# A two-layer graph network on one core: both ends of the kernel are reordered

## What is computed

```
h  = relu(layernorm(x))                                  # x: (128, 128, 64)
hj = relu(h @ W1a [j]  +  (h[j] - h[k]) @ W1b + b1)      # for each edge j-k, 192 wide
x  = x + (sum over k of mask[j,k] * hj) @ W2 + deg[j] * b2
h  = relu(layernorm(x))
x  = x + (adj @ h) @ W^T
```

## Time and profile before

| | |
|---|---|
| median of 3 runs | 842.91 us (841.57 to 843.62) |
| the profiled execution, its own time | 845.98 us |
| its span, first to last instruction | 844.1 us |
| busy share of the span: PE, PEld, DVE, ACT, POOL | 96%, 85%, 96%, 94%, 72% |
| mean granted TensorE clock | 0.98 of full |
| codes | 0 to 46.3 us |
| tables, until `tables_ready` | 46.3 to 52.1 us |
| loop over graphs, first sum to last gather | 56.9 to 827.3 us |
| tail: last steps and the last store | 827.3 to 844.1 us |

### The profile page before, as it was taken

How to read it: one execution, slowest core, us unless ns; L and a number is a source line. 1 busy time by engine, 2 the same in 40 slices (tenths; PEclk the granted TensorE clock), 3 DMA queues, 4 the chain that set the end, 5 groups by cost and what they waited for, 6 DMA issues and landing times.

```text
span 844.1 us, 26648 instructions
## 1 busy us (share of the span) xinstructions
PE 810.6 (96%) x8242; PEld 715.0 (85%) x8243; DVE 809.9 (96%) x2894; ACT 794.9 (94%) x2246; POOL 611.5 (72%) x1174
## 2 busy tenths in 40 slices
PE   4879999999999999999999999999999999999996
PEld 2447888898889888988998899888988898889884
DVE  6969999999999999999999999999999999999993
ACT  4969999999999999999999999999999999999992
POOL 1966777777777777777777777777777777777762
PEclk8979999999999999999999999999999999999996
DMA  9800000000000000000000000000000000000000
GB/s 337 327 1 2 7 9 21 21 21 15 21 20 21 9 21 21 20 15 21 21 21 9 20 21 21 15 21 20 21 9 21 21 20 14 21 21 21 15 3 21
DMA packets 26705, 27.55 MB, mean 33 GB/s; under 512 B 3520, under 2 KB 24512, under 8 KB 25536
## 3 DMA queue, kind: packets, MB, share of 16 engines
q1 hardware_dynamic: 25488, 25.37, 8.9%
q10 hardware_dynamic: 1072, 0.43, 0.2%
HBM read 21.59 MB, written 4.19 MB: 31 GB/s over the span
## 4 chain that ended last, share of the span: by engine, by line
PE 90%; DVE 4%; issue 2%; ACT 2%; DMA 1%; SPq 0%; ACTq 0%; DVEq 0%
PE ring L414 48%; PE ring L442 8%; PE prep L471 5%; PE post L514 4%; PE post L501 3%; PE post L508 3%; PE post L502 3%; PE prep L479 3%; PE prep L482 2%; PE prep L477 2%; DVE acc L826 2%; PE post L506 2%; DMA x_all<-x_nbf_dram 1%; PE prep L473 1%; DVE onehot_space L812 1%
## 5 line engine op out<-in xcount | busy, mean ns | idle before, releaser
L826 DVE SCALAR_TENSOR_TENSOR acc<-ring,acc 128x384 f32<-128x384 f32 x896 | 488.6, 545 | 0.6
L572 ACT COPY ring<-P 128x384 f32<-128x384 f32 x1024 | 466.6, 509 | 19.3 <-DVE acc L826 11.4
L414 PE MATMUL ring<-PQ,onehot_space 128*128 128x192 f16 x4096 | 417.0, 247 | 4.5 <-ACT ring L572 2.2
L414 PEld LDWEIGHTS ring<-PQ,onehot_space 128*128 128x128 f16 x4096 | 328.0, 99 | 39.4 <-issue 13.5
L922 POOL TENSOR_SCALAR start<-P,spare 128x192 f32<-128x192 f32 x128 | 128.4, 1003 | 134.8 <-ACT P L622 133.8
L946 POOL TENSOR_TENSOR row_space<-row_space 128x192 f32<-128x192 f32 x256 | 153.4, 599 | 25.3 <-ACT row_space L610 8.2
L812 DVE TENSOR_SCALAR onehot_space<-mask_all 128x512 f16<-128x512 f16 x512 | 158.1, 311 | 0.0
L442 PE MATMUL ring<-PQ,owner 128*128 128x384 f16 (+1 forms) x512 | 93.9, 306 | 0.0
L414 PE MATMUL ring<-PQ,onehot_row 128*128 128x192 f16 x768 | 84.3, 246 | 0.5 <-DVE onehot_row L874 0.3
L610 ACT ACTIVATE row_space<-ring 128x576 f32<-128x576 f32 x128 | 83.3, 651 | 0.7 <-PE ring L414 0.7
L826 DVE SCALAR_TENSOR_TENSOR acc<-ring,start 128x384 f32<-128x384 f32 x128 | 71.1, 556 | 5.3 <-PE ring L414 1.3
(11 more groups left out here) (138 smaller groups left out, 1431.9 us busy)
## 6 DMA issues: line engine op xcount, KB each, us to landing
onehot_space<-adj_kbj_dram SPq DMA_DIRECT2D x8, 1024.0 KB, 17.3
adj_again<-adj_kbj_dram SPq DMA_DIRECT2D x128, 64.0 KB, 2.0
x_all<-x_nbf_dram SPq DMA_DIRECT2D x8, 512.0 KB, 19.0
out_dram<-x_all SPq DMA_DIRECT2D x32, 128.0 KB, 1.9
consts<-consts_dram SPq DMA_DIRECT2D x1, 192.0 KB, 2.4
scratch<-w1a_dram ACTq DMA_DIRECT2D x2, 48.0 KB, 4.2
scratch<-w1b_dram ACTq DMA_DIRECT2D x2, 48.0 KB, 6.7
scratch<-b_dram ACTq DMA_DIRECT2D x1, 96.0 KB, 10.1
```

What stands on the lines that cost most here:

```text
L414: last = nc.tensor.matmul(to, hot(s), parts[:, part, H:2 * H], start=False, stop=(part == 1), skip_group_check=True)
L572: return nc.scalar.copy(slots[to][:, bank_], src.unsqueeze(1).broadcast_to([N, PER_BANK, H]))
L826: return nc.vector.scalar_tensor_tensor(sums, slots[to][:, bank_], 0.0, start[:, :, :] if first else sums, ALU.max, ALU.subtract if first ...
```

## The change

At the front: TensorE's products for the scale search come later, behind part 2 and part 3 of the codes, and VectorE's and ScalarE's share of the search moves back with them; mask 2 comes ahead of the first maximum. Four ring writes come ahead of the first pair of table products. The first four one-hots are made before VectorE waits for the last codes, and two small operations trade places with waits. ScalarE runs parts 1 to 3 in a loop of the device and does its first two norms ahead of the scaled weights.

In every step: TensorE's wait for `hm_row_ready` stands between the transposes and the product that needs it.

At the tail: in step 128 VectorE, not GpSimd, adds the three slots of the last graph's owned rows. ScalarE makes the two `h2` of the last two pairs together, in the odd step. The last store is split in two.

```diff
-            sp.wait_ge(y_ready, B // 2)
-            sp.dma_start(out[:, B - STORE:B, :], x_all[:, B - STORE:B, :]).then_inc(stored, 16)
-            sp.wait_ge(stored, 16 * B // STORE)
+            for done in range(B - STORE + 2, B + 1, 2):
+                sp.wait_ge(y_ready, done // 2)
+                sp.dma_start(out[:, done - 2:done, :], x_all[:, done - 2:done, :]).then_inc(stored, 16)
+            sp.wait_ge(stored, 16 * (B // STORE - 1 + STORE // 2))
...
             codes(0)
-            codes(1, range(QUADS // 2))
+            codes(1)
+            codes(2)
 
             pe.wait_ge(largest_ready, 1)
             nc.tensor.matmul(post[0:1, 0:N], to_scale[:, 0:1], ident, start=True,
                              stop=True).then_inc(largest_seen, 1)
-            codes(1, range(QUADS // 2, QUADS))
+            codes(3)
             pe.wait_ge(largest_ready, 2)
             nc.tensor.matmul(post[:, N:N + 1], ones_row[:, :], to_scale[0:1, 1:2], start=True, stop=True).then_inc(largest_seen, 1)
-            with pe.Fori(2, LATE) as g:
+            with pe.Fori(EARLY, LATE) as g:
                 codes(g)
...
                             pe.wait_ge(summed, b * REGULAR)
-                            pe.wait_ge(hm_row_ready, b)
                             if not main:
                                 pe.wait_ge(even_T_ready, pairs(b, u, t, -2))
                             for s in range(PER_BANK):
                                 nc.tensor.matmul(head_ps, acc_space[:, (u - 1) // 2 % 2, s, heads[(u - 1) % 2]], ident, start=(s == 0), stop=False, is_transpose=True)
+                            pe.wait_ge(hm_row_ready, b)
                             last = nc.tensor.matmul(head_ps, row_heads[(u - 1) % 2], ownerT[:, (u - 1) % QUAD, :], start=False, stop=True)
...
-            pe.wait_ge(rows_counted, 1)
-            nc.tensor.matmul(tables[:, 0, :], ones[:, :], rows, start=True, stop=True)
-            nc.tensor.matmul(tables[:, 1, :], rows, ones[:, :], start=True, stop=True).then_inc(rows_summed, 1)
...
             pe.wait_ge(code_kj_ready, B // QUAD)
-            pe.wait_ge(code_jk_ready, B // QUAD)
             write_ring(range(QUADS))
+
+            pe.wait_ge(rows_counted, 1)
+            nc.tensor.matmul(tables[:, 0, :], ones[:, :], rows, start=True, stop=True)
+            nc.tensor.matmul(tables[:, 1, :], rows, ones[:, :], start=True, stop=True).then_inc(rows_summed, 1)
...
-                    if i == 4 and exists(b - 5):
+                    if i == 4 and exists(b - 5) and (u % 2 or exists(b - 1)):
...
-                        k, g = (u - 5) // 2 % 2, (u - 5) % 2
-                        nc.scalar.activation(h2[:, k, 2 * g, :], x_all[:, b - 5, :], ACT.Relu, bias=shift2[:, k, g:g + 1],
-                                             scale=rstd2[:, k, g:g + 1]).then_inc(h2_ready, 1)
+                        k = (u - 5) // 2 % 2
+                        for g in range(2) if not exists(b - 1) else ((u - 5) % 2,):
+                            of = b - 5 - (u - 5) % 2 + g
+                            nc.scalar.activation(h2[:, k, 2 * g, :], x_all[:, of, :], ACT.Relu, bias=shift2[:, k, g:g + 1],
+                                                 scale=rstd2[:, k, g:g + 1]).then_inc(h2_ready, 1)
...
             codes(0)
-            codes(1)
-            codes(2)
+            with nc.scalar.Fori(1, EARLY) as g:
+                codes(g)
+            act.wait_ge(norm1_ready, 1)
+            lead(step, hi=-1)
             act.wait_ge(scale_ready, 1)
             nc.scalar.activation(w_parts[:, 0, :, 0:H], w_pq[:, :].rearrange("p (k h) -> p k h", k=3), ACT.Copy,
                                  scale=to_scale[:, 2:3]).then_inc(first_parts_ready, 1)
-            codes(3)
-            act.wait_ge(norm1_ready, 1)
-            lead(step, hi=-1)
...
             norm1_stats(1)
+            mask(2)
             largest()
-            mask(2)
-            largest_of_rows()
             moments(0)
             norm1_stats(2)
-            scale()
             mask(3)
+            largest_of_rows()
             norm1_stats(3)
             moments(1)
             mask(4)
-            second_parts()
+            scale()
             mask(5)
             norm1_stats(4)
+            second_parts()
             mask(6)
...
             moments(3)
+            dve.wait_ge(code_kj_ready, 1)
+            first_hot()
...
-            dve.wait_ge(p_ready, 1)
-            second_part(0, 0)
-
             dve.wait_ge(rows_summed, 1)
...
+            nc.vector.tensor_copy(row_count[:, :], owned)
+            dve.wait_ge(p_ready, 1)
+            second_part(0, 0)
             dve.wait_ge(owned_sums, 1)
             nc.vector.tensor_scalar(loops[0:1, 0, :], tables[0:1, 3, :], float(LOOPED), None, ALU.mult)
-            nc.vector.tensor_copy(row_count[:, :], owned)
...
+                if not main and b == B:
+
+                    dve.wait_ge(relu_row_ready, B)
+                    sums = relu_rows[(u - 1) % 2][:, 0, :]
+                    nc.vector.tensor_tensor(sums, sums, relu_rows[(u - 1) % 2][:, 1, :], ALU.add).then_inc(half_row_ready, 1)
+                    dve.wait_ge(half_row_ready, B)
+                    nc.vector.tensor_tensor(sums, sums, relu_rows[(u - 1) % 2][:, 2, :], ALU.add).then_inc(hm_row_ready, 1)
...
-            for s in range(SLOTS):
-                last = hot(0, 0, 0, s)
-            last.then_inc(onehot_ready, 1)
             lead(step)
...
-                if exists(b - 1):
+                if exists(b - 1) and exists(b):
 
                     pool.wait_ge(relu_row_ready, b)
```

More of the change, by code:

```diff
@@ L371, in _, with codes @@
                     adj(b + BODY + 1)
-            sp.wait_ge(y_ready, B // 2)
-            sp.dma_start(out[:, B - STORE:B, :], x_all[:, B - STORE:B, :]).then_inc(stored, 16)
-            sp.wait_ge(stored, 16 * B // STORE)
+            for done in range(B - STORE + 2, B + 1, 2):
+                sp.wait_ge(y_ready, done // 2)
+                sp.dma_start(out[:, done - 2:done, :], x_all[:, done - 2:done, :]).then_inc(stored, 16)
+            sp.wait_ge(stored, 16 * (B // STORE - 1 + STORE // 2))
         @block.tensor
         def _(pe):
-            def codes(g, quads=range(QUADS)):
+            def codes(g):
                 pe.wait_ge(mask_ready, g + 1)
-                for q in quads:
+                for q in range(QUADS):
                     quad = g * QUADS + q
@@ L753, in moments, with hot, first_hot @@
                 nc.vector.tensor_tensor(mom[:, 3, b], mom[:, 3, b], mom[:, 2, b], ALU.add).then_inc(moments_ready, 1)
+            def hot(b, u, i, s):
+                return nc.vector.tensor_scalar(onehot[:, hot_of(u), i, s, :, :], code_kj[:, bass.ds(b, QUAD), :],
+                                               2.0 * (SLOTS * i + s) + 1.0, None, ALU.is_equal)
+            def first_hot():
+                for s in range(SLOTS):
+                    last = hot(0, 0, 0, s)
+                last.then_inc(onehot_ready, 1)
             mask(0)
@@ L808, in _ @@
             dve.wait_ge(tables_ready, 1)
-            def hot(b, u, i, s):
-                return nc.vector.tensor_scalar(onehot[:, hot_of(u), i, s, :, :], code_kj[:, bass.ds(b, QUAD), :],
-                                               2.0 * (SLOTS * i + s) + 1.0, None, ALU.is_equal)
             def prepare(b, u, s):
```

## The result

The changed kernel takes 846.83 us (median of 8 runs, 845.11 to 849.21) beside 842.77 (8 runs, 841.57 to 844.04) for the kernel before: 1.0038 times as long, 95% interval 1.0024 to 1.0052. I forecast 841.9 with a range to 843.5, so it went the other way: 4.1 us slower where I had 1.05 faster and gave "slower" a chance of 0.06.

What follows compares the result with a forecast made beforehand. TensorE, VectorE and ScalarE, each 94 to 96% busy, were taken as one full pipeline in the middle, with serial ends. Front 0, middle 0 and tail 1.05 gave 842.91 - 1.05 = 841.86, say 841.9 us; range 839.9 to 843.5.

Steps and rivals of the forecast that it cites:

- The middle: Loop over graphs: a full pipeline whose streamed work the change doesn't alter, moved TensorE wait included; gain 0.
- Rival (d): Every step: TensorE's moved wait between transposes and product opens a gap; at 30 ns a step 845.7; chance 0.05.
- Codes: Front: ScalarE's code copies end 1.25 us earlier, group 4 starting at 28.4 instead of 29.56; bounds 0.3 and 2.0.
- T0: Front: the end of ScalarE's last code copy out of PSUM, 46.31 before, forecast 45.05.
- The 2.76 of idle time: Front: ScalarE's standstill until 18.18, while TensorE waits for the largest weight between two halves of code group 1.
- Ring writes ahead of the tables: Front: four TensorE writes take 1.71 us at clock 0.50, making `owned` 1.71 later against T0, `tables_ready` 0.7 later.
- rival (b): Front: ring writes at full clock take 0.86, `start` comes 0.85 earlier; sum about 1.6, 841.3; chance 0.12.
- GpSimd's `start`: Front, graph 1: done at 62.72 instead of 62.26, so VectorE waits and the 1.65 us won are spent.
- The front: Everything ahead of graph 1: gain 0 in sum, bounds -1.0 and 1.65.
- The tail: From step 128: result copy 0.8 us earlier through VectorE's sums, plus 0.25 from the store; 1.05, bounds 0.5 and 1.8.
- pair norms: Tail: ScalarE's paired norms end near 831.9 and 835.4, before the line 599 copies (near 832.9 and 835.8); counted nothing.
- The halved last store: Tail end: last store, 2.6 us from issue to landing, with half the bytes gains 0.25; skill's estimate 0.15.

Runs made afterwards that it cites:

- e1_wait_only: Kernel before with one edit: TensorE's wait for hm_row_ready stands behind the two transposes; 842.86 us, ratio 0.9996 to the kernel before.
- e5_after_one_more: Changed kernel with one VectorE instruction more (first memset written as two halves); 844.11 us, ratio 0.9997 to the kernel before.
- e7_after_two_more: Changed kernel with two VectorE instructions more (first memset in three pieces); 844.32 us, ratio 1.0000 to the kernel before.
- e10_norm_early_singles: Changed kernel, first memset in halves, GpSimd's last first-layer norm group moved earlier, last second-layer norms one by one; 842.71 us, ratio 0.9984 to the kernel before.
- e12_part_later: Kernel before with VectorE's wait for p_ready and the subtraction behind it moved six instructions later; 847.91 us, ratio 1.0049 to the kernel before.
- e8: Changed kernel with three VectorE instructions more (first memset in four pieces); 844.10 us, ratio 0.9992 to the kernel before.
- e3_front_only: Kernel before with all edits of the front and no other; 847.41 us, ratio 1.0042 to the kernel before.
- e4_all_but_wait: Changed kernel with TensorE's wait for hm_row_ready put back ahead of the transposes; 847.36 us, ratio 1.0046 to the kernel before.

## Why the prediction was wrong, step by step

**The middle** was the step that failed: "the change doesn't alter what any engine streams there", so 0. The products and sums are the same, but their places in VectorE's instruction stream are not. The moved wait was rightly 0. The place of the code cost 3.5 us (0.9997 against 1.0038 with one split memset, with an uncertainty of about 1.4), of which the traces show 2.65 in the middle, 762.07 against 759.42; where the rest lies I can't show, and it may be noise. None of my rivals had this mechanism, so the range left it out. Rival (d) named 845.7, near what was measured, but by a gap at TensorE's wait that `e1_wait_only` doesn't show (0.9996); that nearness is chance. The trace of before could not have shown it: there number 63 falls on the wait in front of these sums, and the sums behind it start on time.

**Codes.** I said T0 would come 1.25 earlier, at 45.05. It came at 45.78, 0.53 earlier:

```profile
19.20 0.59 ACT L568 CAST mask_all<-ring 128x512 f32 x1 [2.00 <-PE ring L392]
...
23.60 0.59 ACT L568 CAST mask_all<-ring 128x512 f32 x1 [0.38 <-PE ring L392]
...
28.76 0.64 ACT L568 CAST mask_all<-ring 128x512 f32 x1
...
33.41 0.59 ACT L568 CAST mask_all<-ring 128x512 f32 x1 [0.34 <-PE ring L392]
...
45.09 0.69 ACT L569 CAST code_jk<-ring 128x512 f32 x1
```

The 2.76 of idle time didn't go; 2.00 of it moved behind group 1, to the wait for mask 2's data, as I had said it would. Group 3 began at 23.60, where I had 23.25, and group 4 at 28.76, where I had 28.4: mask 3 was late by 0.22 and TensorE by the rest. I had then taken 0.15 of the later stalls back; instead one grew, to 0.34 at 33.41, and 0.27 of the 0.80 won by group 4 was lost by 45. The mechanism was right and the size 2.4 times too large, inside my bounds. Over all traces the last copy ends at 46.3 to 46.7 with the old front and at 45.8 to 47.1 with the new one (middle values 46.6 and 46.1), so 0.5 is the typical gain, and two single executions need not show it.

**Ring writes ahead of the tables.** I had 1.71 for them at a granted clock of 0.50. From the last code copy to `owned` the kernel before takes 3.13 (46.31 to 49.44), `e5_after_one_more`, where the clock was at half for the whole stretch, 4.79 (46.68 to 51.47), that is 1.66 more: right for that clock. Five others lie between, at 4.12 to 4.65. But the profiled execution of the changed kernel took 3.09, with its writes at the full clock:

```profile
46.48 1.03 PE L533 MATMUL ring<-code_jk,ident_h 128*128 128x512 f16 x4
47.35 0.39 PE L540 MATMUL ring<-scratch,ones 128*128 128x128 f32 x2
```

That is rival (b), with 1.03 for the four writes where I had halved 1.71 to 0.86, and `e7_after_two_more` shows it too (3.09). I had given it 0.12 on the 0.50 of one trace; two of the eight traces with this order of the writes have it. The Trainium skill, "TensorE: Matmul & The Clock Gate", section "Part 1: The HAM clock gate", says that the moment of a clock change is not tied to the kernel's start; the traces agree: the same writes met the full clock in two of eight.

**GpSimd's `start`.** I had it done at 62.72 and VectorE idle before it. In `e7_after_two_more` it is done at 62.70:

```profile
61.77 0.93 POOL L937 TENSOR_SCALAR start<-P,spare 128x192 f32<-128x192 f32 x1
62.73 0.56 DVE L837 SCALAR_TENSOR_TENSOR acc<-ring,start 128x384 f32<-128x384 f32 x1 [1.19 <-POOL start L937]
```

(the second row is VectorE's), and in the profiled execution of the changed kernel 61.41, with the same 1.19 of idle time behind it. From `owned` to its end are 12.82 before and 12.54 after. The front came out as I had it, with 0 as its sum, as far as such a scatter can show: over the six kernels with the changed front and the norm at its old place graph 1 begins at 61.44 to 64.10 us (middle value 62.8), over the six with the old front at 62.28 to 63.15 (62.6).

**The tail.** VectorE's two sums took what I had said, 0.36 each where I had 0.35, and TensorE's product follows them and not GpSimd:

```profile
829.67 0.36 DVE L845 TENSOR_TENSOR row_space<-row_space 128x192 f32<-128x192 f32 x1 [1.09 <-ACT row_space L611]
830.06 0.36 DVE L847 TENSOR_TENSOR row_space<-row_space 128x192 f32<-128x192 f32 x1
...
830.48 0.49 PE L504 MATMUL post<-ownerT,row_space 128*128 128x128 f32 x2 [1.06 <-DVE row_space L847]
```

From the first sum of graph 127 to ScalarE's copy of the result are 8.89 before and 8.16 after: 0.73 of the forecast 0.8. (In the forecast's own sum 828.8 + 1.1 is 829.9, not 829.95; that changes nothing.) But of this not all reaches the end, because of the pair norms, which I had priced at nothing. ScalarE of the changed kernel:

```profile
835.77 0.77 ACT L632 ACTIVATE h<-x_all,shift,rstd 128x64 f32<-128x64 f32 x2 [1.93 <-POOL shift L998]
836.45 0.24 ACT L600 COPY sums_T<-post 128x128 f32<-128x128 f32 x1
```

and of `e1_wait_only`, with single norms:

```profile
833.99 0.44 ACT L629 ACTIVATE h<-x_all,shift,rstd 128x64 f32<-128x64 f32 x1 [1.60 <-POOL shift L985]
834.33 0.24 ACT L599 COPY sums_T<-post 128x128 f32<-128x128 f32 x1
```

The copy that TensorE needs comes 0.68 behind the start of the norms instead of 0.34. In both the clock was still full there; at half clock, as in the trace that I had read, the copy waits for TensorE: `e10_norm_early_singles`, with single norms, shows ScalarE idle for 0.65 ahead of it, in which the second norm's 0.34 would be hidden. My 0.4 of margin was a margin of the half clock. And TensorE's clock moves the tail more than any of its edits does. It fell to half 8.8 us behind the first sum of graph 127 in the trace of before, and the tail took 22.2. In `e1_wait_only`, with the same tail code, it fell 14.0 behind, and the tail took 20.1; the changed tail takes 19.3 to 20.3 where it falls 12.8 to 15.5 behind. The second and the third stretch of 5 us from that sum on, in the kernel before and then in `e1_wait_only` (length; busy time of PE, PEld, DVE, ACT and POOL; granted clock, DMA share, GB/s):

```profile
826.90:831.90 5.00, 2.58 (x21) 2.26 (x19) 0.93 (x6) 1.69 (x4) 2.50 (x6) 0.88 0.00 0
831.90:836.90 5.00, 3.85 (x15) 2.99 (x14) 1.18 (x6) 1.33 (x5) 1.32 (x4) 0.50 0.08 28
```

```profile
826.20:831.20 5.00, 2.84 (x25) 2.44 (x23) 0.92 (x6) 1.79 (x4) 2.51 (x6) 1.00 0.00 0
831.20:836.20 5.00, 2.91 (x16) 2.18 (x16) 1.47 (x7) 1.54 (x5) 1.32 (x4) 0.90 0.09 30
```

Like against like, the changed tail is worth 0.1 to 0.5 us at the full clock, not the 1.05 that I took from a half-clock trace (20.1 to 20.3 against 20.6 where the clock falls about 13 behind, 19.9 to 20.0 against 20.1 to 20.2 at 14 to 15). At half clock, with single norms, it was 1.0, as forecast: 20.9 for `e10_norm_early_singles` against 21.9 for `e12_part_later`, with the clock down 9.3 behind in both. The halved last store gave less than my 0.25: it lands 2.1 to 2.5 us after its issue in the eight traces that have it, the whole one 2.4 to 2.6 in six (2.6 in the earlier trace rows), 0.1 less in the mean. The prediction's estimate of 0.15 for it, by the Trainium skill, "DMA: Bandwidth & Descriptors", section "Anatomy of one DMA", is nearer; the section gives its figures for transfers that GpSimd issues, and this one is SyncE's.

**The sum as it should have been:** 0 for the front, some 0.3 won in the tail, and about 3.5 lost to the place of VectorE's code: 3.2 slower, where 4.1 was measured, with an uncertainty of 1.2. Without the last term, as in `e5`, `e7` and `e8`, the change makes no difference that can be told: 0.9992 to 1.0000.

## What to carry to other kernels

In an unrolled kernel whose engines are full, an edit ahead of the loop moves all code behind it. Here one instruction fewer on VectorE cost 0.3 to 0.5% without changing any work. So compare the count of instructions on each engine, separate waits included, before believing a result below 0.5%, and try the kernel again with one, two and three cheap instructions more. A wait can add to that count or not, by where it stands: here, behind another wait it was an instruction, and behind a copy it was none. And read a serial tail or front at both levels of TensorE's clock before pricing an edit there: what has a margin at half clock may be the chain at full clock.

## What the runs showed of the hardware

- A first sum that is number 63 of a run of 128 VectorE instructions (counted in the trace from the program's first, separate waits included) starts about 0.35 us late: 19 of 19. The same is not shown for every number 63: of 251 other operations with this number in the loop, 5 start 0.20 to 0.23 late (all of them sums behind `owner`) and the rest as usual. Whether something hides the lateness there I can't show.
- The transfers of instructions on queue 14 are 8 KB each (0.62 MB in 76), which is 64 bytes for each of 128 instructions, and they keep step with VectorE's count: over the 14 traces one begins within 1 us behind number 62 in 82% of the runs of 128 in the loop, where the mean over all numbers is 9%. In `e3_front_only` one begins 0.67 us behind each of the four late sums. That the lateness is VectorE going over to the next block of its code is what these fit; it was not shown by itself. Transfers follow one place in ScalarE's and GpSimd's count too (53% behind number 62, 64% behind number 67), but whether these engines start anything late there is open.
- A delay of 0.35 on VectorE can grow or be won back. In 13 of the 19 cases the step behind it is 0.4 to 0.6 longer as well (6.53 instead of 5.93 in step 29 of the changed kernel), since `from_first` and `onehot_row` then take 0.60 and 0.87 instead of 0.24 and 0.40, and TensorE waits for them. In five the step behind is 0.3 shorter (5.62 or 5.63), and in one it is as usual. So the traced middle lost between 1.5 us (`e4_all_but_wait`) and 2.8 (`e12_part_later`). Why the two operations take longer, collisions with GpSimd or another cause, was not tested.
- The moment at which TensorE's clock falls to half in the tail lay from 8.5 to 15.5 us behind the same instruction in 14 traces. With the same code in the tail it took 22.2 us where the clock fell at 8.8 and 20.1 where it fell at 14.0, a larger difference than any edit of the tail made.
